# The B row of each scan state: a broadcasting DMA into SBUF in place of a bf16 product into PSUM

## What is computed

```
x_dbl = einsum('bld,ed->ble', u, x_proj_w)
dt, Bm, Cm = split(x_dbl, [DT_RANK, DT_RANK + D_STATE])
dt = softplus(dt @ dt_proj_w.T + dt_proj_b);  A = -exp(A_log)
def step(h, inputs):                       # over the sequence
    dA = exp(dt_t[:, :, None] * A)
    h = dA * h + (dt_t * u_t)[:, :, None] * B_t[:, None, :]
    y = einsum('bdn,bn->bd', h, C_t)
```

## Time and profile before

| what | value |
|---|---|
| device time, median of 3 runs | 2605.71 us (2605.02 to 2606.45) |
| span of the profiled execution, first to last instruction | 2602.9 us |
| setup, until the first state starts | about 75 us |
| scan stage, 24 chunks | about 75 to 1188 us, 46.4 us a chunk |
| expert stage | about 1188 to 2603 us |

### The profile page before, as it was taken

The page is one execution under the profiler, slowest core; times in us unless marked ns, Lnnn a source line. Parts: engine busy times, 40 slices in busy tenths (PEclk is TensorE's granted clock), DMA queues, the critical chain, the costliest instruction groups (busy, mean ns, idle before and its releaser), DMA issues.

```text
span 2602.9 us, 28352 instructions
## 1 busy us (share of the span) xinstructions
PE 2384.9 (92%) x7648; PEld 1242.0 (48%) x7649; DVE 1314.5 (51%) x2016; ACT 1018.9 (39%) x2041; POOL 1232.4 (47%) x1086
## 2 busy tenths in 40 slices
PE   4788989888898898888999999999999999999995
PEld 3445545555455554544444444444444444444443
DVE  1899999999999999992321111111111111111112
ACT  3777877778777787762110111101111101111110
POOL 2889999999999999983051000011111111111110
PEclk8999999999999999999999999999999999999997
DMA  4122222222222222221003000331313132231116
GB/s 173 52 72 64 80 71 74 77 65 81 71 74 77 65 80 71 77 73 56 29 25 122 21 28 23 113 121 24 121 24 115 31 121 90 55 121 24 24 20 154
DMA packets 69266, 186.07 MB, mean 71 GB/s; under 512 B 10080, under 2 KB 15304, under 8 KB 66336
## 3 DMA queue, kind: packets, MB, share of 16 engines
q1 hardware_dynamic: 57424, 160.06, 18.8%
q0 software_dynamic: 11728, 24.73, 5.1%
HBM read 158.14 MB, written 26.62 MB: 71 GB/s over the span
## 4 chain that ended last, share of the span: by engine, by line
PE 53%; ACT 15%; issue 12%; POOL 8%; DVE 6%; DMA 4%; SPq 0%; POOLq 0%; ACTq 0%; DVEq 0%
PE pair L1497 29%; PE single L1509 16%; ACT WALL L819 6%; DVE WALL L1062 3%; DMA u<-xrows,gix 2%; POOL WALL L566 2%; PE pair L1373 2%; POOL dtu L470 1%; POOL dt L463 1%; POOL dt L466 1%; DVE pair L1050 1%; PE pair L1479 1%; ACT L665 1%; ACT L673 1%; PE pair L1520 1%
## 5 line engine op out<-in xcount | busy, mean ns | idle before, releaser
L1497 PE MATMUL pair<-WALL,z 128*128 (+1 forms) x1952 | 849.9, 593 | 3.0 <-ACT z L881 3.0
L566 POOL TENSOR_TENSOR WALL<-WALL 128x768 f32<-128x768 f32 x384 | 694.1, 1821 | 66.0 <-PE pair L1373 43.7
L1062 DVE TENSOR_TENSOR_SCAN WALL<-WALL,carry,pair 128x384 f32<-128x384 f32 x640 | 610.3, 993 | 0.1
L1497 PEld LDWEIGHTS pair<-WALL,z 128*128 128x128 f32 x1952 | 366.8, 190 | 442.5 <-issue 440.9
L1373 PE MATMUL pair<-WALL,ident 128*128 128x384 f32 x1536 | 560.0, 489 | 1.6 <-DVE pair L1050 1.0
L819 ACT ACTIVATE WALL<-dt,An 128x384 f32<-128x384 f32 x768 | 421.5, 605 | 140.9 <-POOL dt L466 136.4
L887 ACT ACTIVATE dt<-pair 128x512 f32<-128x512 f32 x122 | 72.9, 597 | 813.9 <-PE pair L1497 813.9
L1373 PEld LDWEIGHTS pair<-WALL,ident 128*128 128x128 f32 x1536 | 284.2, 192 | 149.7 <-issue 23.1
L1189 DVE SCALAR_TENSOR_TENSOR dtu<-dt,tab,pair 128x512 f32<-128x512 f32 x86 | 64.3, 747 | 549.0 <-ACT dt L887 549.0
L1198 DVE COPY absx<-pair 128x512 f32<-128x512 f32 x61 | 42.2, 692 | 393.6 <-PE pair L1520 393.6
L1509 PE MATMUL single<-WALL,absx 128*128 (+1 forms) x488 | 221.7, 597 | 2.9 <-issue 1.8
(11 more groups left out here) (228 smaller groups left out, 2257.3 us busy)
## 6 DMA issues: line engine op xcount, KB each, us to landing
WALL<-crows SPq DMA_DIRECT2D x192, 384.0 KB, 3.5
WALL<-in_L_ffn_w_dram SPq DMA_DIRECT2D x24, 2048.0 KB, 13.8
X<-in_x_dram SPq DMA_DIRECT2D x4, 1152.0 KB, 6.6
xrows<-rows SPq DMA_DIRECT2D x24, 192.0 KB, 3.5
u<-xrows SPq DMA_DIRECT2D x18, 256.0 KB, 2.7
WALL<-yrows SPq DMA_DIRECT2D x4, 1152.0 KB, 15.6
out_dram<-X SPq DMA_DIRECT2D x8, 576.0 KB, 10.5
WALL<-in_L_ffn_sw_dram SPq DMA_DIRECT2D x2, 2048.0 KB, 17.0
```

The costliest lines, as they stand in the source:

```text
L566: pool.tensor_tensor(hC[m], hs[:, (NS * j + n) % HRING, :, :], Cs[G % 3][:, n % CG, :].unsqueeze(1).to_broadcast([P, HALF, T]), ALU.mult). ...
L1062: scan = nv.tensor_tensor_scan(hs[:, m, h, :], dA[(NS * j + n) % AHEAD][:, h, :], dBu[h], init, ALU.mult, ALU.add)
L1497: last = mm(bank[2 * w + q][:, :], xT[k][:, r, :], WALL[:, ds(off + (w * RR * I + r * I + q * 512), 512)], start=(r == 0), stop=(r == RR - 1))
```

## The change

The product `spread`, the selector `sel`, the three-part rows `S`, the residue `Rm` and all that makes them (`bc_hi`'s bf16 copy, `bc_mid`, `residue`, `low_part`) go. SP stores all 32 B and C rows of a chunk to DRAM and loads the B row of each state with a DMA that broadcasts it to 128 partitions, into a ring `Bs` of four rows in SBUF. DVE's `dBu` products read `Bs` in place of the PSUM bank, and wait for the DMA in place of PE. The setup is shortened in the same way: one fp32 product with `ident` stands for 16 products with `sel` for the token's state.

```diff
-    RK = 3 * BC
+    RK = BC
+    BRING = 4
...
-        S = [sb(f"S{k}", [3 * BC, T], bf16) for k in range(2)]
-        Rm = sb("Rm", [2 * BC, T])
+        Bs = sb("Bs", [P, BRING, T])
...
+            def load_b(g, k, n):
+
+                sp.dma_start(Bs[:, n % BRING, :],
+                             bcrows[k, n:n + 1, :].to_broadcast([P, T])).then_inc(m_B[n % BRING], 16)
...
+                        for n in range(q * CG, (q + 1) * CG):
+                            if not (first and NS * j + n < BRING):
+                                sp.wait_ge(m_dBu, NS * g + n - BRING + 1)
+                            load_b(g, k, n)
                         if not (first and G < 3):
                             sp.wait_ge(m_hC, NS * g + CG * (q - 2))
...
-                        if q == NS // CG - 2 and not (last and j == JC - 1):
-                            store_c(g + 1, 1 - k)
+                        if q == NS // CG - 3 and not (last and j == JC - 1):
+                            store_bc(g + 1, 1 - k)
...
-            for q in range(3):
-                pool.wait_ge(s_const, 5 + q)
...
-                pool.affine_select(out=sel[:, :, :], in_=sel[:, :, :], compare_op=ALU.not_equal, fill=1.0,
-                                   base=-BC * q, pattern=[[-1, NS], [0, P]], channel_multiplier=1)\
-                    .then_inc(s_const, 1)
...
-            def low_part(g, k):
-                pool.wait_ge(f_mid, g + 1)
-                pool.tensor_tensor(S[k][0:BC, :], Rm[0:BC, :], S[k][0:BC, :], ALU.subtract).then_inc(f_lo, 1)
...
-                nsc.activation(S[k][:, :], M0[0:3 * BC, 0:T], ACT.Copy).then_inc(f_hi, 1)
...
-                        v.wait_ge(m_B, i + 1)
+                        v.wait_ge(m_B[n % BRING], 16 * ((NS // BRING) * g + n // BRING + 1))
...
-                        nv.tensor_tensor(dBu[0], dtu[k][:, 0, :], Bb[n % 2][:, 0:T], ALU.mult).then_inc(m_dBu0, 1)
+                        nv.tensor_tensor(dBu[0], dtu[k][:, 0, :], Bs[:, n % BRING, :], ALU.mult).then_inc(m_dBu0, 1)
                         after(v, m_h, i)
-                        nv.tensor_tensor(dBu[1], dtu[k][:, 1, :], Bb[n % 2][:, 0:T], ALU.mult).then_inc(m_dBu, 1)
+                        nv.tensor_tensor(dBu[1], dtu[k][:, 1, :], Bs[:, n % BRING, :], ALU.mult).then_inc(m_dBu, 1)
...
-                        if front and n == 5:
-                            residue(g + 1, 1 - k)
...
-            def spread(g, j, n):
-                mm(Bb[n % 2][:, 0:T], sel[:, n, :], S[j % 2][:, :], start=True, stop=True).then_inc(m_B, 1)
```

More of the change, by code:

```diff
@@ L186, in bass_metaformer_mamba_moe_kernel @@
         f_dt, f_dtu = sem("f_dt"), sem("f_dtu")
-        m_B = sem("m_B_in_psum")
+        m_B = [sem("m_B_loaded" + str(r)) for r in range(BRING)]
         m_dA = sem("m_dA")
         m_C = [sem("m_C_loaded" + str(r)) for r in range(3)]
-        f_cr, f_cst = sem("f_c_rows_copied"), sem("f_c_rows_stored")
+        f_cr, f_cst = sem("f_bc_rows_copied"), sem("f_bc_rows_stored")
         m_dBu0, m_dBu = sem("m_dBu_half0"), sem("m_dBu")
@@ L254, in bass_metaformer_mamba_moe_kernel @@
         NLOAD = [0]
-        NCONST = 9
+        NCONST = 5
         def weights_of(q, ws):
@@ L544, in _ @@
             sequence(1, 1)
-            low_part(0, 0)
             front_centre(2, 0, 2)
@@ L578, in batch @@
                                 normalise(g - 2)
-                        if front and n == 6:
-                            low_part(g + 1, 1 - k)
                         if front:
@@ L684, in silu_z, with bc_rows @@
                 nsc.activation(z[r][:, :, :], z[r][:, :, :], ACT.Silu).then_inc(f_z, 1)
-            def bc_hi(g, k):
+            def bc_rows(g):
                 sc.wait_ge(f_bcps, g + 1)
-                after(sc, m_B, NS * (g - 1))
-                nsc.activation(S[k][:, :], M0[0:3 * BC, 0:T], ACT.Copy).then_inc(f_hi, 1)
                 after(sc, f_cst, 16 * g)
@@ L694, in bc_hi @@
                 nsc.activation(dtr[:, :], M0[RK:RK + RANK, 0:T], ACT.Copy).then_inc(f_rank, 1)
-            def bc_mid(g, k):
-                sc.wait_ge(f_res, g + 1)
-                nsc.activation(S[k][0:2 * BC, :], Rm[:, :], ACT.Copy).then_inc(f_mid, 1)
             def abs_relu(g):
@@ L998, in centre @@
                                  ALU.subtract).then_inc(done, 1)
-            def residue(g, k):
-                v.wait_ge(f_hi, g + 1)
-                v.wait_ge(f_cr, g + 1)
-                v.wait_ge(f_rank, g + 1)
-                after(v, f_mid, g)
-                after(v, f_lo, g)
-                nv.tensor_tensor(Rm[:, :], M0[0:2 * BC, 0:T], S[k][0:2 * BC, :], ALU.subtract).then_inc(f_res, 1)
             def gate_y(g, r):
@@ L1020, in _ @@
                 front_variance(g, bank[2 + g][:, 0:CP])
-            residue(0, 0)
             v.wait_ge(s_x, 16 * (B - 1))
@@ L1265, in _ @@
             last.then_inc(s_setup, 1)
-            pe.wait_ge(s_setup, SETUP + 17)
-            for n in range(NS):
-                last = mm(M0[:, 16 + n:17 + n], sel[:, n, :], S[1][:, 0:1], start=True, stop=True)
-            last.then_inc(s_setup, 1)
+            pe.wait_ge(s_setup, SETUP + 14)
+            mm(M0[:, 16:16 + NS], bcrow[0:NS, 0:P], ident[0:NS, 0:NS], start=True, stop=True).then_inc(s_setup, 1)
             def mean_of(x4, done, ps):
@@ L1379, in add_skip @@
                 last.then_inc(m_du, 1)
-            pe.wait_ge(f_lo, 1)
-            for n in range(2):
-                spread(0, 0, n)
             def batch(b, first, last):
```

83 lines of the change are left out of this document (32 added, 51 removed).

## The result

| | device time, median (range), us |
|---|---|
| before | 2606.08 (2605.02 to 2608.70) |
| after | 3154.18 (3151.74 to 3155.90) |

The ratio is 1.210, 95% interval 1.208 to 1.212: the change costs 548 us. The forecast was 3225 in a range from 2800 to 3360.

The account below looks back on a forecast made before the run. DVE was taken as the bound, 98% busy in the scan stage. Holds of 678 us, less 45, residue -11 and setup -2 gave +620 on 2605.7, stated as 3225 us, range 2800 to 3360.

Parts of the forecast that it names:

- DVE is the bound and pays every wait in full: Scan stage: DVE busy 98%, POOL close behind at 92%, so anything DVE waits for is paid in full.
- `hC` goes between the two products: Each state on DVE: first product 0.45, `hC` 1.77, second product and scans 2.29, in sum 4.51 us; chance 0.45.
- the pair goes together whenever `hC` is waiting: Rival: DVE keeps the memory over both products, `hC` waits 0.91 us; 2900, 2870 or 2760 us; chance 0.36 including mixtures.
- One of the signs: Expected in the changed trace's scan stage: PE near half busy, beside a 4.5 us state and POOL with idle time.
- The hold is a whole POOL step of 1.77 us: Upper bound for one `dBu` product, taken wherever a POOL step is in the way; the lower bound was nothing.
- The 0.14 us by which POOL lets go early: Under the pair-together rival: POOL frees memory before its recorded end, up to 4.6 us off a chunk, giving 2760 us.
- All 383 states are held: Scan stage: 383 states with an `hC` before them, each held 1.77 us, 678 us in all.
- the term of -45: At n = 10 and 12 a shorter residual or centre step replaces `hC` in the gap: 45 us less over 22 chunks.
- `hC` starts 0.16 us after the first product: Read at one place: first product at 642.75, `hC` at 642.91; the second product would start at 0.45 us.
- The clock: PE's granted clock, 0.85 in the setup, may fall when PE waits half a state: another 70 us as a guess.
- Residue -11, setup -2, the relief of PE, POOL and ACT nothing: DVE's dropped residue gains 11 us, the setup 1.6; work removed from PE, ACT and POOL counts nothing.
- The loads are hidden: B rows issued 10.5 us ahead of need, counted as nothing; rival of a late row: 2755 us, little for it.

Follow-up runs that it names:

- run that forced it: The changed kernel with POOL's `hC` also waiting for the second product of the next state; 2871.24 us, ratio 1.101.
- run with both rows in PSUM: The changed kernel with all its loads and waits, but both products read a constant row in PSUM instead of the B row; 2583.08 us, ratio 0.991.

## Why the prediction was right, and where its sizes were off

- *DVE is the bound and pays every wait in full.* Right: it is busy 99.7% of the stage, and 579 us more of products gave 551 us more of span.
- *`hC` goes between the two products.* Right, and it is seen in the second product's median of 2.165 us beside 537 ns of the first. The rival, that the pair goes together whenever `hC` is waiting, showed only in the run that forced it. One of the signs did not come: PE was to be near half busy in the scan stage, and is busy for 68% of it.
- *The hold is a whole POOL step of 1.77 us.* Too large. At 704.38 the second product takes 2.17 where 0.55 is its own time, so the hold is 1.62 us: it had its operands at 706.00, and POOL's recorded end is 706.13. The 0.14 us by which POOL lets go early, here 0.13, stood among the rivals, read from L944, and belonged in the main sum: 383 x 0.15 = 57 us.
- *All 383 states are held.* Wrong, with an error on the other side. The second products' excess of 481 us is that of 481 / 1.62 = 297 full holds; in fact 289 were held in full, 45 in part and 50 not at all. Where one is missing, as at 722.39, `hC` came late (there after PE) and ran beside the scans. The forecast had no term for first products, and they were held for 98 us. The forecast of 678 - 45 = 633 us became 579: of the 54 us, the size of the hold is 57, and the missed holds, the first products and the term of -45 nearly cancel. That they cancel is luck; so is part of the nearness of 3225 to 3154.
- *`hC` starts 0.16 us after the first product, so before the second.* It starts within 0.45 us of it in 227 of 383 states of the changed kernel, but not for the reason given: in the kernel before, from one place of which it was read, it does so in 49. The change itself brings it about, by holding DVE until POOL has to wait for the scans.
- *The clock.* The granted clock fell to 0.85 in the stage, from 0.99, and PE's readout L1336 took 584 ns against 489, as guessed. A price for it beside the holds does not show in the sums above. POOL's waits for that readout rose from 43.7 to 80.3 us; whether the clock made them longer, or PE's own waits for DVE's products, is not shown.
- *Residue -11, setup -2, the relief of PE, POOL and ACT nothing.* Residue and setup are as forecast. PE's relief is not nothing: the gate `yd` of the kernel before had waited 7.1 us for PE's readout (first row below), and no longer does (second row, the kernel after). The run with both rows in PSUM gained 23 us, some 10 more than the 13 forecast; its gate still waited for 3.0 us (third row), so 4 of them are this, and the rest stays unassigned.

```profile
L1014 DVE TENSOR_TENSOR yd<-pair,z 128x768 f32<-128x768 f32 x24 | 22.9, 956 | 7.2 <-PE pair L1373 7.1
```

```profile
L987 DVE TENSOR_TENSOR yd<-pair,z 128x768 f32<-128x768 f32 x24 | 22.7, 945 | 0.0
```

```profile
L988 DVE TENSOR_TENSOR yd<-pair,z 128x768 f32<-128x768 f32 x24 | 22.9, 956 | 3.0 <-PE pair L1340 2.6
```

- *The loads are hidden.* Right: 3.5 us to landing, no wait of DVE, and the run with the loads alone.

From 620 forecast to 551 in the spans, then: 54 us less of holds, 7 us of the gate; about 8 us stay unassigned.

## What to carry to other kernels

A DVE product of two tensors beside a POOL that computes on SBUF, as measured here, wants one of its inputs in PSUM: what it costs otherwise is the rest of the POOL instruction that runs when it comes up, so ask which one that is, and how long, state by state. The order in time of the kernel before is no sure guide to that, since the holds themselves shift it. It need not be the operand that changes; here the one that is constant for 16 states was the cheap one to put there (one ACT copy a chunk). Then look in the copying engine's order at what stands ahead of the copy: in one instruction, behind four decays and a square, it cost 122 us more than in two halves ahead of them. (Both were changed at once; a half is ready at most 0.4 us sooner than the whole of 0.80 us, 10 us in 24 chunks, so nearly all of it is the place.)

## What was not expected of the hardware

- Two back-to-back DVE instructions are let through one at a time: a POOL instruction that comes up during the first (704.25 against 703.93) gets in ahead of the second, although that one starts 0.45 us after the first. (The Trainium skill, SBUF — State Buffer, section Who interferes with whom, has it that the second to start blocks until the first is finished; the 1.62 us agree with a hold of nearly the whole instruction.)
- An instruction that is held so shows it in its own duration and not as idle time: `hC` has a median of 2.04 us here, against 1.80 when nothing is in its way (723.33), and the held second products have 0.0 us of idle time before them.
- On DVE, in the run with the second product behind the first scan, a scan right behind the product that it reads starts 0.58 to 0.68 us after that product's start, 0.11 to 0.23 us later than one that waits for an earlier product (0.45 to 0.47).
